# A macaron block on one core: late slots and attention's last products in another order, the later norms scaled by ScalarE

## What is computed

```
def _layernorm(x, axis=-1, eps=1e-05):
    m = jnp.mean(x, axis=axis, keepdims=True)
    v = jnp.var(x, axis=axis, keepdims=True)
    return (x - m) / jnp.sqrt(v + eps)
...
    x = x + 0.5 * _L0_ffn_ref(_layernorm(x, axis=-1), ...)
    x = x + _L0_attn_ref(_layernorm(x, axis=-1), L0_attn_w_qkv, L0_attn_w_dense)
    x = x + 0.5 * _L0_ffn_ref(_layernorm(x, axis=-1), ...)
    return x
```

```
        attn = jnp.einsum('bkgst,btkd->bskgd', probs, vh)
        attn = attn.reshape(Bq, Sq, NHEADS * HEAD_D)
        return attn @ w_dense.T
```

## Time and profile before

| | |
|---|---|
| timed runs (3) | median 1137.86 us, from 1136.82 to 1140.55 |
| the profiled execution | 1148.46 us |
| its span, first to last instruction | 1146.7 us |
| its mean granted TensorE clock | 0.989 of full speed |
| TensorE busy in it | 1095.6 us (96%) |
| VectorE, ScalarE, GpSimd busy | 795.0, 633.2, 545.4 us |

### The profile page before, as it was taken

The page is one execution under the profiler, slowest core; times in us unless marked ns, Lnnn a source line. Parts: engine busy times, 40 slices in busy tenths (PEclk is TensorE's granted clock), DMA queues, the critical chain, the costliest instruction groups (busy, mean ns, idle before and its releaser), DMA issues.

```text
span 1146.7 us, 22418 instructions
## 1 busy us (share of the span) xinstructions
PE 1095.6 (96%) x6584; PEld 945.2 (82%) x6584; DVE 795.0 (69%) x2145; ACT 633.2 (55%) x1729; POOL 545.4 (48%) x540
## 2 busy tenths in 40 slices
PE   8979999899999999999999999999999988979996
PEld 6767877688998988888899888898889976768875
DVE  7668868766666666667667666676766778568866
ACT  4247753465656646646555655564755653247750
POOL 1536648165346336427426535634642530536644
PEclk9989999999999999999999999999999999989999
DMA  9986666100200200200010010020010006935556
GB/s 356 415 302 206 188 206 195 52 1 1 93 2 1 92 0 0 77 14 0 37 55 0 15 76 0 0 91 0 0 37 2 1 4 275 383 101 174 187 164 203
DMA packets 38622, 114.85 MB, mean 100 GB/s; under 512 B 4384, under 2 KB 4384, under 8 KB 36512
## 3 DMA queue, kind: packets, MB, share of 16 engines
q1 hardware_dynamic: 33440, 97.30, 23.5%
q0 software_dynamic: 5120, 16.78, 4.3%
HBM read 79.20 MB, written 34.87 MB: 99 GB/s over the span
## 4 chain that ended last, share of the span: by engine, by line
PE 77%; DVE 8%; issue 5%; ACT 4%; another core or an unknown queue 2%; DMA 2%; POOL 1%; DVEq 0%; POOLq 0%; ACTq 0%; SPq 0%
PE bank L1581 20%; PE bank L1615 13%; PE bank L1706 9%; PE bank L1648 8%; PE bank L1556 7%; PE bank L1594 5%; PE bank L1567 4%; PE bank L1470 3%; PE bank L1517 2%; PE bank L1702 1%; PE bank L1644 1%; DVE x L1191 1%; DVE x L1109 1%; POOL yg L593 1%
## 5 line engine op out<-in xcount | busy, mean ns | idle before, releaser
L611 POOL TENSOR_TENSOR scores<-scores,pinv 128x512 f32<-128x512 f32 (+3 forms) x256 | 181.9, 742 | 217.7 <-DVE pinv L1296 217.7
L1198 DVE TENSOR_TENSOR pT_lo<-bank,pT_hi 128x512 fp32r<-128x512 f32 (+2 forms) x192 | 100.9, 553 | 85.1 <-ACT pT_hi L842 84.9
L554 POOL TENSOR_TENSOR tback_lo<-experts,tback_hi 128x768 fp32r<-128x768 f32 x62 | 114.2, 1844 | 83.6 <-ACT tback_hi L749 83.6
L871 ACT ACTIVATE scores<-scores,nmax 128x512 f32<-128x512 f32 (+3 forms) x256 | 140.5, 561 | 0.0
L1263 DVE CUSTOM_DVE_ANT_0 scores<-bank,causal 128x512 f32<-128x512 f32 (+3 forms) x256 | 112.2, 485 | 1.5 <-issue 0.4
L842 ACT ACTIVATE pT_hi<-bank 128x512 fp32r<-128x512 f32 (+2 forms) x192 | 86.9, 488 | 45.4 <-PE bank L1594 45.4
L1581 PE MATMUL bank<-xnT_hi,wqs_hi 128*128 128x512 f32 x256 | 102.7, 401 | 0.0
L1581 PE MATMUL bank<-xnT_lo,wqs_hi 128*128 128x512 f32 x256 | 101.3, 396 | 0.0
L1581 PE MATMUL bank<-xnT_hi,wqs_lo 128*128 128x512 f32 x256 | 101.2, 395 | 0.0
L1594 PE MATMUL bank<-ident,scores 128*128 128x128 f32 x640 | 90.9, 273 | 0.3 <-POOL scores L611 0.3
L1594 PEld LDWEIGHTS bank<-ident,scores 128*128 128x128 f32 x640 | 75.5, 141 | 9.3 <-POOL scores L611 0.5
(11 more groups left out here) (240 smaller groups left out, 3514.6 us busy)
## 6 DMA issues: line engine op xcount, KB each, us to landing
experts<-in_ffn_w SPq DMA_DIRECT2D x32, 768.0 KB
xn<-x_rows SPq DMA_DIRECT2D x62, 256.0 KB, 2.7
y_rows<-xn SPq DMA_DIRECT2D x62, 256.0 KB, 2.0
raw_q<-in_wq SPq DMA_DIRECT2D x8, 1024.0 KB
raw_d<-in_wd SPq DMA_DIRECT2D x8, 1024.0 KB
x_rows<-experts SPq DMA_DIRECT2D x1, 7936.0 KB, 30.4
raw_w<-in_ffn_w SPq DMA_DIRECT2D x8, 768.0 KB, 5.3
raw_kv<-in_wkv SPq DMA_DIRECT2D x8, 512.0 KB, 3.4
```

What stands on the lines that cost most here:

```text
L554: nc.gpsimd.tensor_tensor(tback[par][1][:], experts[:, bass.ds(at + FRONT, GU - FRONT)], tback[par][0][:].bitcast(F32), ALU.subtract).then ...
L611: nc.gpsimd.tensor_tensor(s, s, pinv[k % 2][:, i:i + 1].to_broadcast([P, P * (i + 1)]), ALU.mult).then_inc(att.normed, 1)
L871: nc.scalar.activation(s, s, ACT.Exp, bias=nmax[par][:, i:i + 1], scale=-1.0, accum_out=psumr[par][:, i:i + 1]).then_inc(att.exp, 1)
L1198: nc.vector.tensor_tensor(pT[1][:, lo_col:hi_col], bank[b][:, 0:hi_col - lo_col], pT[0][:, lo_col:hi_col].bitcast(F32), ALU.subtract).then ...
```

## The change

It has four parts. (1) The norms 1 and 2 are scaled by ScalarE: VectorE ends the short chain with one more 128x4 instruction, −mean · rstd, and ScalarE writes xn = rstd · x + that, as an activation Identity with two per-partition operands. (2) The pass m = 0 of `combine(0, 4)` moves ahead of norm 1's first low halves. (3) In each late slot VectorE does the addition to x first, then s2's low half and left_sum; s1's and s3's low halves go behind the query's. (4) At attention's end, part of the product s2 moves ahead of a12's second part, and VectorE's and ScalarE's work for norm 2 is placed between the additions; three products wait for fewer additions, or for none.

The core of the diff:

```diff
+            def scaled(n, h):
+
+                act.wait_ge(norm[n].var, 2 * h + 2)
+                for t in range(HALF * h, HALF * h + HALF):
+                    nc.scalar.activation(xn[:, t, :], x[:, t, :], ACT.Identity, bias=newt[:, t:t + 1],
+                                         scale=rstd[:, t:t + 1]).then_inc(norm[n].mul, 1)
...
+                    if isinstance(u, int) and u == UNITS:
+                        roots(2, 0)
                     if exists(u, 1, UNITS):
                         turned_hi(u - 1, 2, COL[2], COL[3], 6)
...
                     if exists(u, 1, UNITS):
                         heads(g, k)
+                    if isinstance(u, int) and u == UNITS:
+                        scaled(2, 0)
...
                 act.wait_ge(att.proj_mm, PROJ_AHEAD + 1)
+                scaled(1, 1)
                 value(0)
                 turned_norm(1, 1)
...
                 roots(2 * n, 1)
+                if n == 1:
+                    scaled(2 * n, 1)
                 cut_dn(n, 0)
...
                 high(n, SLOTS - 1)
+                if n == 0:
+                    scaled(1, 0)
...
                 for t in range(HALF * h, HALF * h + HALF):
+                    if (n, t) == (2, HALF + 2):
+                        between()
+                        dve.wait_ge(att.added, NP * 2 * KV)
...
+                if n:
+                    nc.vector.scalar_tensor_tensor(out=newt[:, part], in0=mv[:, part, 0], scalar=-1.0, in1=rstd[:, part],
+                                                   op0=ALU.mult, op1=ALU.mult).then_inc(s.var, 1)
+                    return
...
-                    if late:
-                        left_lo(g, k - 1, "s2", first_o[:, 0:2 * P])
                     if r and todo and exists(u, 0, UNITS):
                         add_product(todo.pop(0), b=(k - 5) // 4 % 2)
                     if late:
-                        left_lo(g, k - 1, "s1", first_o[:, 2 * P:])
-                        left_lo(g, k - 1, "s3", o_diff[:])
+                        left_lo(g, k - 1, "s2", first_o[:, 0:2 * P])
                         left_sum(first_o[:, 0:2 * P], bank[1][:, 0:2 * P], first_o[:, 0:2 * P], ALU.subtract)
...
                     if isinstance(u, int) and u > UNITS:
-                        todo = todo[1:]
+                        adds = {product[0]: product for product in todo}
+                        left_lo(g, k - 1, "s1", first_o[:, 2 * P:])
+                        add_product(adds["a12"], b=1)
+                        add_product(adds["s2"], b=1)
+                        left_lo(g, k - 1, "s3", o_diff[:])
+                        add_product(adds["s1"], b=1)
                         left_lo(g, k - 1, "s4", first_o[:, 0:2 * P])
-                        add_product(todo.pop(0), b=1)
-                        scaled(2, 0, norm_then)
-                        for _ in range(3):
-                            add_product(todo.pop(0), b=1)
-                        turned_norm(2, 0)
+                        turned_norm(2, 0, 0, 2)
+                        add_product(adds["s3"], b=1)
+                        turned_norm(2, 0, 2, HALF)
+                        add_product(adds["s4"], b=1)
+                        norm_then = statistics(2, 1, lambda: add_product(adds["a22"], b=1))
+                        return
...
-                    if late and exists(u, 0, UNITS):
+                    if isinstance(u, int) and u == UNITS - 1:
+                        add_product(todo.pop(0), b=0)
+                    if late:
+                        left_lo(g, k - 1, "s1", first_o[:, 2 * P:])
+                        left_lo(g, k - 1, "s3", o_diff[:])
                         left_lo(g, k - 1, "s4", first_o[:, 0:2 * P])
                     for product in todo:
                         add_product(product, b=(k - 5) // 4 % 2)
+                    if isinstance(u, int) and u == UNITS:
+                        scaled(2, 0, norm_then)
...
             low(0, SLOTS - 1)
+            combine(0, 4, (0,))
             turned_norm(1, 0)
-            combine(0, 4)
+            combine(0, 4, (1,))
...
-                        pe.wait_ge(att.added, NP * (2 * KV - 1) + (LAST.index(chain[-1]) + 1 if chain else 0))
+                        if chain:
+                            pe.wait_ge(att.added, NP * (2 * KV - 1) + LAST.index(chain[-1]) + 1)
+                        elif i == "a12":
+                            pe.wait_ge(att.added, NP * (2 * KV - 2) + PRODUCTS.index("a12") + 1)
+                        else:
+                            pe.wait_ge(att.masked, 4 * UNITS)
...
                     if isinstance(u, int) and u > UNITS:
+                        dense(todo[LAST.index("s2")], g, k, (0,))
                         for product in todo[1:]:
...
-                            dense(product, g, k, (1,) if product[0] in ("a12", "s1") else (0, 1))
+                            dense(product, g, k, (1,) if product[0] in ("a12", "s1", "s2") else (0, 1))
```

More of the change, by code:

```diff
@@ L667, in roots @@
             def roots(n, h):
-                act.wait_ge(norm[n].var, h + 1)
+                act.wait_ge(norm[n].var, (h + 1, 2 * h + 1, 2 * h + 1)[n])
                 part = slice(HALF * h, HALF * h + HALF)
                 nc.scalar.activation(root[:, part], rvar[:, part], ACT.Sqrt).then_inc(norm[n].root, 1)
+            def scaled(n, h):
[3 more added lines that the diff above has]
+                                         scale=rstd[:, t:t + 1]).then_inc(norm[n].mul, 1)
             def turned_norm(n, h):
@@ L883, in slot @@
                         query(bank[0])
-                    if isinstance(u, int) and u == UNITS:
-                        roots(2, 0)
                     if exists(u, 1, UNITS):
                         heads(g, k)
+                    if isinstance(u, int) and u == UNITS:
+                        scaled(2, 0)
                     if r in (1, 3) and exists(u, 2, UNITS - 5):
@@ L958, in _, with statistics @@
         def _(dve):
-            def statistics(n, h):
+            def statistics(n, h, between=None):
                 s = norm[n]
@@ L973, in statistics @@
                 if n == 2:
-                    dve.wait_ge(att.added, NP * (2 * KV - 1 + h))
+                    dve.wait_ge(att.added, NP * (2 * KV - 1) + (LAST.index('s4') + 1 if h else 0))
                 for t in range(HALF * h, HALF * h + HALF):
+                    if (n, t) == (2, HALF + 2):
+                        between()
+                        dve.wait_ge(att.added, NP * 2 * KV)
                     if n == 0 and t % 2 == 0:
@@ L1005, in normalise, with turned_norm @@
                 scaled(n, h, statistics(n, h))
-            def turned_norm(n, h):
+            def turned_norm(n, h, first=0, last=HALF):
                 s = norm[n]
-                for t in range(HALF * h, HALF * h + HALF):
+                for t in range(HALF * h + first, HALF * h + last):
                     dve.wait_ge(s.hi, t + 1)
@@ L1179, in routed, with combine @@
                 tile_steps(step)
-            def combine(n, t):
-                for m in range(2):
+            def combine(n, t, parts=(0, 1)):
+                for m in parts:
                     for tile in (t, t + 1):
@@ L1341, in attention, with feed_forward @@
                 att_tail(slot, 1, 1)
-            def feed_forward(n):
+                return norm_then
+            def feed_forward(n, norm_then):
                 if n == 0:
@@ L1347, in feed_forward @@
                     low_gu(n, 0)
-                normalise(2 * n, 1)
+                    normalise(2 * n, 1)
+                else:
+                    scaled(2 * n, 1, norm_then)
                 if n == 0:
@@ L1372, in feed_forward @@
                 add_down(n, SLOTS - 2)
-            feed_forward(0)
+            feed_forward(0, None)
             then = statistics(1, 0)
@@ L1378, in _ @@
             low(0, SLOTS - 1)
+            combine(0, 4, (0,))
             turned_norm(1, 0)
-            combine(0, 4)
+            combine(0, 4, (1,))
             combine(0, 6)
             add_down(0, SLOTS - 1)
-            attention()
-            feed_forward(1)
+            feed_forward(1, attention())
             multiply(1, SLOTS - 1)
```

1 line of the change is left out of this document (added).

## The result

The changed kernel is slower: 1172.68 us (median of 4 runs, 1169.81 to 1176.02) beside 1138.14 us of the kernel before (with a fourth run beside the three above), a ratio of 1.0294 (95% interval 1.027 to 1.0318), 34 us. The forecast was 1137.0 us.

The account below looks back on a forecast made before the run. TensorE, busy 96% of the span, was taken as the bound, so only its waits could be won. Terms −2.05 + 0.45 + 1.6 − 0.9 = −0.9 us, from 1137.86 to 1137.0 us; range 1133.0 to 1139.5.

Parts of the forecast that it names:

- Rival (b): Attention loop: three low halves in GpSimd's stretch eat more than the slack; slower, about +6, 1143 us; chance 0.08.
- (c): Attention loop: the wait stays, s2's low half waiting behind GpSimd's next piece; 0 instead of −2.05, 1139.1 us; chance 0.1.
- The loop's addition: Attention loop: putting the addition to x first removes six TensorE waits of 0.34 us; −2.05 us.
- The first group: Loop's first group: 1.12 us gained at first_o is given back at pT_lo, and 0.5 more; +0.45 us.
- The low halves in GpSimd's stretch: Attention loop: moved s1 and s3 subtractions make ScalarE's first_o copy 0.2 to 0.7 us later, within 1.06 slack; nothing.
- The norm of attention: Norm 1: ScalarE makes xn at 0.83 us, step 0.72, so turns and copies end later; +1.6 us, range +0.6 to +1.9.
- Attention's end: After the loop: s2 matmuls fill a gap, xn comes earlier, last product 1.9 us earlier; −0.9 us, range −2.2 to −0.4.

Follow-up runs that it names:

- experiment 1: Changed kernel with six one-column VectorE MEMSETs, writing to a small added tile, ahead of its first instruction; 1135.51 us, 0.9964 of the kernel before.
- experiment 5: Kernel before with only the late slots' new order, up to the slot behind unit 63; 0.999 of the kernel before.
- wait6: Changed kernel with six VectorE instructions that only wait ahead of its first, no new tile; 1138.75 us, 0.9994 of the kernel before.
- norm1_dve: Changed kernel with norm 1 back on VectorE and no padding; 1.0004 of the kernel before.
- b_loop: Same run as experiment 5: kernel before with only the late slots' new order; 0.999 of the kernel before.
- pad3: Changed kernel with three one-column VectorE MEMSETs ahead of its first instruction; 1169.23 us, 1.0285 of the kernel before.
- b_norm1: Kernel before with norm 1 alone scaled by ScalarE, no padding; 1174.05 us, 1.0311 of the kernel before.
- experiment 2: Same run as pad3: changed kernel with three VectorE MEMSETs ahead of its first instruction; 1169.23 us, 1.0285 of the kernel before.
- experiment 3: Same run as pad5: changed kernel with five VectorE MEMSETs ahead of its first instruction; 1133.69 us, 0.9954 of the kernel before.
- experiment 4: Same run as b_norm1: kernel before with norm 1 alone scaled by ScalarE; 1174.05 us, 1.0311 of the kernel before.
- experiment 6: Same run as norm1_dve: changed kernel with norm 1 back on VectorE, no padding; 1.0004 of the kernel before.
- experiment 9: Same run as wait6: changed kernel with six VectorE instructions that only wait ahead of its first; 1138.75 us, 0.9994 of the kernel before.
- experiment 10: Kernel before with an unused tile of 32 bytes a partition ahead of the large tiles; 0.998 of the kernel before.
- experiment 11: Kernel before with an unused tile of 64 bytes a partition ahead of the large tiles; 0.9993 of the kernel before.
- best: Kernel before with late slots' order, attention's end with norm 2 on ScalarE, and the 32-byte tile; norm 1 on VectorE; 1134.23 us, 0.9955.
- experiment 12: Same run as best: late slots' order, attention's end and 32-byte tile on the kernel before, norm 1 on VectorE; 1134.23 us, 0.9955.
- pad5: Changed kernel with five one-column VectorE MEMSETs ahead of its first instruction; 1133.69 us, 0.9954 of the kernel before.
- pad6: Same run as experiment 1: changed kernel with six VectorE MEMSETs ahead of its first instruction; 1135.51 us, 0.9964 of the kernel before.
- b_t32: Same run as experiment 10: kernel before with an unused 32-byte tile ahead of the large tiles; 0.998 of the kernel before.

## Why the prediction was wrong

**The step that failed** is the one that isn't in the sum: every edit was costed by what its instructions do, and none by what their number does to the code behind them. "Four VectorE instructions xn … become one" was a duration for me; it was also two times three places in VectorE's list. The loop's body then lay across an edge in the list, and VectorE stood still for 5.3 to 6.4 us at every back edge. In the trace that is 735.7 − 703.1 = 32.6 us over five back edges, 6.5 each: by the rows above 4.7 us of TensorE's wait and 1.7 us of lower clock. In the time it is 1.0294 − 0.9994 of 1138 us, 34 us. None of my rivals had this mechanism. Rival (b) gave the right sign by a mechanism that experiments 1 and 5 refute. (Two of the rivals' totals are off by their own terms: (b) adds up to 1144.0 us and not 1143, (c) to 1139.0 and not 1139.1. Nothing hangs on it.)

**With the loop's place put right the total agrees, in part by luck.** The forecast was −0.9 us; wait6 measures −0.7 us (interval −2.6 to +1.3). That interval can't tell the forecast from no change at all, and the terms below miss on both sides: the loop and attention's end gained more than forecast, norm 1 cost more. By its terms:

- *The loop's addition, −2.05:* right, 0.33 us in each of six groups; with the first group it is −2.1 for the whole loop in three pairs of kernels.
- *The first group, +0.45:* too high. Four units on, the change is 0.1 us behind, and eight units on 0.1 us ahead. The mechanism is there. Rows of wait6:

```profile
246.99 0.83 DVE L1244 TENSOR_TENSOR left_s_lo<-first_o,left_s_hi 128x256 fp32r<-128x256 f32 x1
...
247.91 0.60 ACT L833 ACTIVATE first_o<-bank 128x512 f32<-128x512 f32 x1 [2.45 <-DVE left_s_lo L1244]
...
255.40 0.38 PE L1747 MATMUL bank<-pT_hi,vv_hi 128*128 128x256 f32 x1 [0.79 <-DVE pT_lo L1219]
```

The third low half takes 0.83 us beside GpSimd, ScalarE's copy waits for it, and TensorE's wait for pT_lo is 0.79 us where it was 0.28.
- *The low halves in GpSimd's stretch, nothing in the loop:* right. No wait came that a late copy would make, and none for s2's low half (rival c). ScalarE's copies of first_o waited longer for the low halves (21.1 us in nine waits from 225 to 930 us in wait6, 8.0 in seven before), where there was slack.
- *The norm of attention, +1.6:* too low by the profiles, by how much is open. By wait6 and the two profiles of before it is +2.8 to +4.3. Over all fourteen profiles the seven with norm 1 on VectorE take 27.1 to 30.3 us and the seven with ScalarE 30.1 to 32.4, 2.6 more in the mean. The timed runs don't show it: norm1_dve has 1.0004 and wait6 0.9994. The duration was right:

```profile
L677 ACT ACTIVATE xn<-x,newt,rstd 128x512 f32<-128x512 f32 x16 | 11.7, 803 | 3.7 <-PE bank L1624 2.5 <-DVE newt L1018 1.3
```

803 ns, and four in 2.93 us are a step of 0.71 us. By the figures of the Trainium skill, page "ScalarE: Activation LUTs", section "What ACT_TABLE_LOAD costs", an estimate is 799 ns and a step of 706; the runs agree. What I left out is the clock. In wait6 TensorE waits 1.93 us and then turns tiles at ScalarE's slower pace, and the granted clock falls:

```profile
190.00:193.00 3.00, 2.89 (x15) 2.59 (x16) 1.45 (x3) 3.00 (x7) 2.66 (x3) 0.65 0.63 190
193.00:197.00 4.00, 4.00 (x18) 3.31 (x17) 4.00 (x7) 1.15 (x3) 2.80 (x4) 0.84 0.45 120
197.00:201.00 4.00, 4.00 (x19) 3.22 (x18) 4.00 (x8) 0.77 (x2) 0.00 (x0) 1.00 0.85 351
```

3 × 0.35 + 4 × 0.16 = 1.7 us. In the kernel before these stretches were at 1.00. But this is not the mark of ScalarE's norm: b_loop, with the norm on VectorE, has 0.90 and 0.68 from 193 to 201 us behind a wait of 3.20 us, and pad3 and b_norm1, with it on ScalarE, stay at 1.00 behind waits of 2.05 and 1.90 and still take 30.1 and 30.9 us. So the clock widens the scatter, and what the rest of the norm's cost is stays open.
- *Attention's end, −0.9 with the last stage:* the last product comes 0.9 to 2.6 us earlier after the loop, by the stages above; the forecast had 1.9. There is also a wait I did not see, 2.62 us in wait6:

```profile
935.41 2.47 DVE L996 BATCH_NORM_STATS2 stats<-x 128x6 f32<-128x512 f32 x4
...
938.50 1.12 DVE L1219 TENSOR_TENSOR pT_lo<-bank,pT_hi 128x512 fp32r<-128x512 f32 x2
...
939.21 0.55 PE L1629 MATMUL bank<-ident,scores 128*128 128x128 f32 x3 [2.62 <-DVE pT_lo L1219]
...
943.28 0.36 PE L1655 MATMUL bank<-right_b_hi,left_a_hi 128*128 128x256 f32 x1 [0.87 <-issue]
```

VectorE does the four statistics in front of the pT_lo behind which TensorE's turns wait; before, they came at the same place but TensorE arrived later and did not wait. The wait for xn at 951.58 is gone and the 1.60 us gap is 0.87. What the last stage adds is open: in the second batch it is 6 us longer for both kernels with the new end (196.5, 195.1) than for those without (189.4, 189.7); in the first and third batches and the changed kernel it scatters from 180.6 to 185.5 us with either end. I did not try that apart.

**Shown and not shown.** Shown: the place of VectorE's loop in its list decides over 34 us (experiments 1 to 4, 6, 9), and the edge lies more than three and at most five instructions behind the head of the changed kernel's body. Shown too: the 32-byte tile is worth 4.5 us of the loop, from its second unit on (experiment 10). Argued only: that the blocks are 256 instructions and two of them stay; the runs show one edge, not its period, and that edge, at 697 or 698 of the built list, is no multiple of 256; what the chip has ahead of that list no run shows. Open: the address rule (experiment 11), what the norm costs, the last stage, and the 3 us that `best` fell short.

## What to carry to other kernels

Count each engine's instructions ahead of a loop and in it before you trust a schedule, not only their durations: a loop body of 312 instructions ran without a stall at one place and with two at every back edge six instructions earlier. Before costing an edit, look in the profile's page at the packets of the instruction queue and whether the loop fetches at all; a loop that doesn't can lose that by an edit anywhere ahead of it. Here five or six empty instructions ahead of the loop put it right and three did not, so try a few numbers. To learn what an edit is worth by itself, make the padding of waits: a new tile moves the addresses and changes the time, here by 4.5 us of the loop.

## What the runs showed of the hardware

- With its head at place 693 of VectorE's list a loop body of 312 instructions cost two stalls at each back edge, of 2.5 to 2.7 and of 2.6 to 3.7 us (the changed kernel, b_norm1), at 696 one of 5.7 to 6.5 (pad3), at 698 and 699 none (pad5; pad6 and wait6). At the back edge shown above, transfers at 246 GB/s ran beside the second stall, and TensorE lost 1.7 us more by a granted clock of 0.64 behind it.
- An unused tile of 32 bytes a partition, which moves the large tiles from 32 behind a multiple of 64 to a multiple of 64, made one form of matmul 391 ns instead of 396 and the loop, from unit 2 on, 692.4 us instead of 696.9; with 64 bytes it was 695.2.
- The loop's length in a single profile repeated within 0.05 us (705.21, 705.26; 703.12, 703.14, 703.12), while the medians of the same kernels are known to 2 us. For an edit in such a loop one profile tells more than a dozen timed runs, if its first unit is looked at: in b_t32 a granted clock of 0.65 there added 1 us (8.31 to 9.26).
